# Two adds of the scores go from GpSimd to VectorE in a gated slot attention layer between two feed-forward layers

## The reference, cut to what matters

```python
x = hidden_states                                   # 4 x 512 x 512, float32
x = x + 0.5 * ffn(layernorm(x))                     # three-valued weights, hidden width 1408
x = x + attention(layernorm(x))                     # 16 heads, 128 slots per head
x = x + 0.5 * ffn(layernorm(x))

# attention, for each batch and head, with keys, queries, values, slot weights w, gates g
def step(Sk, Sv):
    Sk = Sk * exp(g)[None, :] + k[:, None] * (beta * w)[None, :]
    Sv = Sv * exp(g)[:, None] + (beta * w)[:, None] * v[None, :]
    s = (q @ Sk) * SCALE
    o = softmax(s) @ Sv
```

## Time and profile before

| | us |
|---|---|
| median of three runs | 2809.32 |
| lowest, highest | 2806.68, 2809.95 |
| the profiled execution | 2808.98 |
| its span, first to last instruction | 2807.1 |
| TensorE busy | 2757.3 |
| VectorE busy | 2229.9 |
| ScalarE busy | 1671.3 |
| GpSimd busy | 1425.0 |

### The profile page before, as it was taken

The page is one execution under the profiler, slowest core; times in us unless marked ns, Lnnn a source line. Parts: engine busy times, 40 slices in busy tenths (PEclk is TensorE's granted clock), DMA queues, the critical chain, the costliest instruction groups (busy, mean ns, idle before and its releaser), DMA issues. The chain is left out here.

```text
span 2807.1 us, 43427 instructions
## 1 busy us (share of the span) xinstructions
PE 2757.3 (98%) x13814; PEld 1933.3 (69%) x13814; DVE 2229.9 (79%) x5777; ACT 1671.3 (60%) x3777; POOL 1425.0 (51%) x2122
## 2 busy tenths in 40 slices
PE   7999999999999999999999999999999999999999
PEld 5887566666666666666666666666666666666887
DVE  7554588988888899888888888888889888884543
ACT  5111677677777677776777677677677777760110
POOL 0200466666566666665666666656666666660000
PEclk9999999999999999999999999999999999999999
DMA  4500211111112111111121111111212111105000
GB/s 169 195 16 28 66 36 35 35 50 35 50 35 69 52 57 35 50 35 49 35 72 50 57 35 51 33 50 35 72 51 60 35 50 38 51 24 199 15 16 30
DMA packets 90932, 151.06 MB, mean 54 GB/s; under 512 B 9297, under 2 KB 30929, under 8 KB 90193
## 3 DMA queue, kind: packets, MB, share of 16 engines
q1 hardware_dynamic: 90704, 148.29, 16.8%
HBM read 127.02 MB, written 21.23 MB: 53 GB/s over the span
## 5 line engine op out<-in xcount | busy, mean ns | idle before, releaser
L1552 PE MATMUL ps<-hT,space 128*128 128x512 f32 x2048 | 996.1, 594 | 1.1 <-ACT hT L1023 1.1
L902 POOL TENSOR_TENSOR s<-s,tmp 128x256 f32<-128x256 f32 (+1 forms) x448 | 367.2, 820 | 302.7 <-DVE tmp L1219 281.4
L1552 PEld LDWEIGHTS ps<-hT,space 128*128 128x128 f32 x2048 | 345.9, 191 | 194.8 <-issue 167.6
L902 POOL TENSOR_TENSOR X<-S,D 128x256 f32<-128x256 f32 x384 | 275.9, 718 | 108.6 <-ACT S L1077 82.5
L1596 PEld LDWEIGHTS ps<-Y,S 128*128 128x128 f32 x1536 | 220.8, 191 | 151.3 <-issue 133.7
L333 ACT ACTIVATE sig<-up_ps 128x512 f32<-128x512 f32 x88 | 52.7, 599 | 406.7 <-PE up_ps L542 406.5
L542 PE MATMUL up_ps<-h_hi,wq 128*128 128x512 f32 x704 | 281.1, 399 | 2.2 <-DVE h_lo L404 2.1
L1584 PEld LDWEIGHTS ps<-AM,XT 128*128 128x128 f32 x1536 | 216.5, 191 | 94.6 <-issue 90.1
L902 POOL TENSOR_TENSOR Y<-aT,D 128x256 f32<-128x256 f32 x384 | 280.5, 752 | 0.0
L542 PE MATMUL up_ps<-h_lo,wq 128*128 128x512 f32 x704 | 278.3, 395 | 0.0
L902 POOL TENSOR_TENSOR A<-ident,dg 128x512 f32<-128x512 f32 x64 | 66.6, 1041 | 390.0 <-DVE space L1296 384.2
(11 more groups left out here) (187 smaller groups left out, 6383.2 us busy)
## 6 DMA issues: line engine op xcount, KB each, us to landing
space<-in_wk_dram SPq DMA_DIRECT2D x64, 256.0 KB, 2.6
space<-in_ww_dram SPq DMA_DIRECT2D x64, 256.0 KB, 2.6
space<-in_wq_dram SPq DMA_DIRECT2D x64, 256.0 KB, 2.7
space<-in_wv_dram SPq DMA_DIRECT2D x64, 256.0 KB, 2.7
space<-in_wo_dram SPq DMA_DIRECT2D x64, 256.0 KB, 3.2
wq_dram<-wq SPq DMA_DIRECT2D x3, 2816.0 KB, 19.4
space<-in_w_dram SPq DMA_DIRECT2D x8, 704.0 KB, 10.9
x_sb<-in_x_dram SPq DMA_DIRECT2D x4, 1024.0 KB, 5.4
```

Source lines behind the costliest of these rows:

```text
L902: return nc.gpsimd.tensor_tensor(out, in0, in1, op)
L1552: mm = nc.tensor.matmul(bank[x][:, :], ck_(slot[x], kk), hT[n // NH % 2][:, kk, :], start=(kk == 0), stop=(kk == KT - 1))
```

## The change

The steps `adst` and `ad64` leave GpSimd's order and stand on VectorE, right behind `m64`, with the same operands. VectorE waits there for GpSimd's `ad32`. TensorE's wait ahead of `sT` is for VectorE's `ad64`.

```diff
-DVE_LATE = ("m16 am64 m32 mst m64 sx0 sx1 sx2 sx3 mx nms dg0 ...
+DVE_LATE = ("m16 am64 m32 mst m64 adst ad64 sx0 sx1 sx2 sx3 mx nms dg0 ...
-POOL_LATE = "ad8 ad16 ad32 adst ad64 a2d y2 y4 y8 r1 y16 y32 y64 yst r2 r3 r4 r5".split()
+POOL_LATE = "ad8 ad16 ad32 a2d y2 y4 y8 r1 y16 y32 y64 yst r2 r3 r4 r5".split()

@@ GpSimd, turn(u)
                     add_level(32, pool_late)
-                    pool.wait_ge(dve_late, after(DVE_LATE, "mst", u))
-                    pool.wait_ge(pool_late, after(POOL_LATE, "ad32", u))
-                    tt(s[:, P:T], s[:, P:T], tmp[2][:, :], ALU.add).then_inc(pool_late, 1)
-                    pool.wait_ge(dve_late, after(DVE_LATE, "m64", u))
-                    pool.wait_ge(pool_late, after(POOL_LATE, "adst", u))
-                    add_level(64, pool_late)

@@ VectorE, turn(u)
                     level_scores(64, dve_late)
+                    dve.wait_ge(pool_late, after(POOL_LATE, "ad32", u))
+                    dve.wait_ge(dve_late, after(DVE_LATE, "mst", u))
+                    tt(s[:, P:T], s[:, P:T], tmp[2][:, :], ALU.add).then_inc(dve_late, 1)
+                    dve.wait_ge(dve_late, after(DVE_LATE, "adst", u))
+                    tt(targets(s, 64), targets(s, 64), by_target(tmp[LEVELS[1:].index(64) % 2], 64),
+                       ALU.add).then_inc(dve_late, 1)
                 if early and 0 <= n % NH - STATS_FROM < C:
                     row_stats(n // NH + 1, n % NH - STATS_FROM)

@@ TensorE, turn(u)
-                    pe.wait_ge(pool_late, after(POOL_LATE, "ad64", u))
+                    pe.wait_ge(dve_late, after(DVE_LATE, "ad64", u))
                     transpose("sT", lambda c: ck_(s, c), pe_late)
```

More of the change, by code:

```diff
@@ L610 @@
             "am1 am2 vr p128 am4 am8 m2 St1 m4 am16 St2 m8 am32").split()
-DVE_LATE = ("m16 am64 m32 mst m64 sx0 sx1 sx2 sx3 mx nms dg0 dg1 dg2 dg3 rs a2_1 a2_2 a2_4 a2_8 a2_16 a2_32 "
+DVE_LATE = ("m16 am64 m32 mst m64 adst ad64 sx0 sx1 sx2 sx3 mx nms dg0 dg1 dg2 dg3 rs a2_1 a2_2 a2_4 a2_8 a2_16 a2_32 "
             "a2_64 oss on oge og").split()
 POOL_EARLY = "x1 b1 bne b2 bnp b4 b8 bn b16 b32 b64 zero ad2 ad4".split()
-POOL_LATE = "ad8 ad16 ad32 adst ad64 a2d y2 y4 y8 r1 y16 y32 y64 yst r2 r3 r4 r5".split()
+POOL_LATE = "ad8 ad16 ad32 a2d y2 y4 y8 r1 y16 y32 y64 yst r2 r3 r4 r5".split()
 BLOCK = [0, 2, 1, 3]
```

## The result

The changed kernel took 2815.8 us (median of 9 runs, 2814.07 to 2817.11), the kernel before 2807.95 (median of 9, 2806.68 to 2809.95): ratio 1.0027, 95% interval 1.0016 to 1.0037, so 4.5 to 10.4 us slower. Forecast was 2818.5, in a range of 2811 to 2824. The profiled execution after has a span of 2814.0 us against 2807.1, 6.9 us longer.

The account below looks back on a forecast made before the run. TensorE, busy 98% of the span, was taken as the bound. Losses of 7.0 us in turns with statistics and 3.0 with normalised rows, less 0.8 in the last turn, made +9.2 us: 2818.5 us, range 2811 to 2824.

Parts of the forecast that it names:

- The bound: TensorE is busy 98% of the span, so other engines' idle time counts only where it makes TensorE wait.
- GpSimd's side: GpSimd loses two adds a turn; the freed time is idle before a wait that doesn't move, so nothing is gained.
- VectorE held 0.93 us: Behind `m64`, the two adds make VectorE free 1.27 us after its start instead of 0.34.
- Plain turns: Load of `sT` 0.09 us later, with 0.05 of margin left; VectorE's idle time hides both adds, length unchanged.
- Turns with statistics: 16 turns with bn_stats and bn_aggr before the tap of `k`: tap 0.61 us late, `aT` costs 0.44 each, 7.0 in all.
- Turns with normalised rows: 8 turns with two tensor_scalar before the tap of `k`: tap 0.53 us late, loss 0.38 net each, 3.0 in all.
- The last turn: Without projections the chain is open; VectorE's adds end sooner than GpSimd's, so `sT` gains 0.8 us, once.
- The sum: Over the whole run: 7.0 + 3.0 - 0.8 = +9.2 us, giving a median of 2818.5 us.
- A: Rival: VectorE has room for the adds at `aT`, only gains of 1.3 us are left, 2808.0 us; chance 0.09.
- B: Rival, half price: the dependent add overlaps or statistics slip partly into covered time, 2.6 us less, 2815.9; chance 0.14.
- C: Rival: VectorE's adds end 0.13 us later than worked out, so `sT` is late as well, 2822 to 2826; chance 0.12.
- D: Rival: the change doesn't reach the path, which only a reordering would do; no chance of its own.

Follow-up runs that it names:

- e4: The kernel before, both adds still on GpSimd, plus two unused products on VectorE behind `m64`, the second waiting for the first: 2817.41 us, ratio 1.0031.
- e2: The kernel before with only the add of level 64 moved to VectorE, the state's add staying on GpSimd: 2808.71 us, ratio 1.0001.
- e5: The changed kernel with only the row statistics moved on VectorE, from behind the two adds to ahead of `m64`: 2811.85 us, ratio 1.0011 to the kernel before.

## Why the prediction was right, step by step

**The bound.** Right in the main: all but about 0.1 us of the change of time were stalls of TensorE at the two places named, `sT` and `aT`. The rest came at a third place, told below under the turns with statistics.

**GpSimd's side.** Right: nothing gained. It has 114 us less work (forecast 115) and no turn is shorter for its freed time. VectorE's two adds take 62.3 us by themselves (forecast 63); its busy time grew by 52, since an add overlaps the end of the step ahead by 0.08 and the normalised rows take 0.41 us less in each of 8 turns.

**VectorE held 0.93 us.** Right within 0.01: from 395.47 to 396.74 are 1.27 us, less the 0.35 it was before. The dependent add starts 0.58 us after a 384-wide one of 0.55, so 0.03 behind its end, as the earlier trace rows had it for `nms`; a start as without a wait would have been at 0.47.

The Trainium skill's sentence that a semaphore costs nothing extra ("VectorE: DVE Perf Modes", "The DRAIN you can't avoid") does not fit this chain: 0.58 against 0.47.

**Plain turns.** Right: load of `sT` 0.12 ahead of its start (forecast 0.1), length unchanged.

**Turns with statistics.** The mechanism was right, the size was not: 0.31 (0.35 to 0.36 in three turns of the first batch) instead of 0.44, 5.1 us instead of 7.0. The term that failed is the lateness of the tap, put at 0.61. It is 0.52: the prediction had VectorE free at the end of bn_aggr, though it is an instruction like others, whose follower without a wait starts ahead of its end; the row shows the tap 0.09 behind the start of the 0.18 us long aggregate. The prediction had read a figure for this overlap, 0.08, and did not use it here. Another 0.03 came back between the tap and `st`: 0.64 us from start to start (397.56, and `st` at 398.20), where a tap that has waited for ScalarE has 0.67 (1409.39, and `st` at 1410.06). So by the unrounded starts the load of `aT` was 0.48 late, less the 0.17 of margin: 0.31.

In the first batch three turns pay 0.04 to 0.06 us more, 0.13 together. The stall at `aT` is 0.31 there too; the rest comes 15 us later, at the transposes of `u_v`, for which TensorE waits in these turns before as well as after. Before and after, in the turn of the earlier trace rows:

```profile
417.07 0.66 PE L1565 MATMUL ps<-ident,u_v 128*128 128x128 f32 x4 [1.34 <-ACT u_v L1067]
...
417.71 0.66 PE L1565 MATMUL ps<-ident,u_v 128*128 128x128 f32 x4 [1.40 <-ACT u_v L1061]
```

The prediction did not look at this hand-over. In e4 it costs the same and in e2 0.03 to 0.05, so it isn't a matter of who hands `sT` over; why this chain comes later by that much more was not followed.

**Turns with normalised rows.** Right: 0.36 each, 2.9 us (forecast 0.38, 3.0). The two steps run at 0.54 us each once GpSimd is idle beside them, the tap comes 0.51 late (forecast 0.53), and the 0.06 at `sT` is gone.

**The last turn.** 0.96 instead of 0.8 gained. The forecast had GpSimd's last two adds at 1.84 us together. They take 2.00 before, counted from the end of the add of level 32: each starts 0.14 us after the end of the one ahead, which the forecast left out, while the last takes 0.72 and not 0.84. VectorE's two take 1.02, as forecast within 0.01.

**The sum.** 5.1 + 2.9 - 0.96 = 7.0 against 9.2, and the spans differ by 6.9. So the two traces are accounted for to 0.1 us. The medians differ by 7.85, and 7.0 lies in the interval of 4.5 to 10.4.

**The rivals.** A (VectorE has the room) is refuted by the 24 turns, and holds in the other 40. The Trainium skill's advice to put elementwise adds on VectorE ("GPSIMD Engine Reference", 4.1 Engine selection) is right on the add's price, 0.55 against 1.00 and 0.43 against 0.79 us. What stands behind the add on that engine decided here. B's figure (2815.9) is the measured one, partly by chance, since the ledger gives 7.0 of the 7.85 us. Its clause "the statistics slip partly into the covered time" is in effect what the overlap behind bn_aggr did; its other reason, an overlap of the dependent add, did not happen. C didn't come: `sT` was in time. D is out, since 24 turns changed their length.

## What to carry to other kernels

When one engine is full, judge a move by the margins of the two or three hand-overs into that engine, in hundredths of a microsecond, and for each kind of turn by itself: here the same two adds were free in 40 turns of 64 and cost 0.31 to 0.36 us in 24. Moving work to the faster engine also moves everything queued behind it there; look for what isn't in every turn, and at every hand-over on which the full engine waits already (`u_v` here). If an engine idles ahead of the place rather than behind it, put the occasional work into that idle time (e5), or split the move (e2).

## What the runs showed of the hardware

- For four transposes of 128 x 128 in float32, TensorE's weight load could begin up to 0.06 us before the multiplications were due without a loss; later cost one for one. It held at `sT` and `aT` in all the kernels (0.08 ahead: free; 0.03 ahead: 0.02 lost; as they were due: 0.06; 0.25 behind: 0.31).
- In this stretch VectorE started the next instruction 0.08 to 0.09 us before the end shown of the one ahead when there was no wait between, after a 0.18 us one too, and 0.03 us behind the end when it waited for it.
- Two tensor_scalar on VectorE (128 x 512, float32) took 1.41 us beside GpSimd's adds and 1.00 us with GpSimd idle; the next instruction started 1.33 and 0.91 us after the first of them. GpSimd's add of level 64 took 0.93 us beside them and 0.72 to 0.73 elsewhere.
